# A decoder of two layers on one core: another order for the steps of part one, and another place for two waits

## The reference, cut to what matters

```
x = norm(x + self_attention(x))          # L0: 16 heads of 8, causal
x = norm(x + cross_attention(x, ctx))    # L0X: 8 heads of 16, 64 keys
x = norm(x + experts(x))                 # router, 64 experts, top 6, 64 places each; shared FFN
x = norm(x + self_attention(x))          # L1: 16 heads of 64, causal, biases on q, k, v
x = norm(x + cross_attention(x, ctx))    # L1X: 16 heads of 64
x = norm(x + nested_attention(x))        # L1F: 8 heads of 16, nested widths 128, 64, 32, 16
```

## Time and profile before

| | |
|---|---|
| median of 3 runs | 1771.91 us |
| lowest, highest | 1770.81, 1782.97 us |
| the profiled execution | 1776.66 us |
| its span, first to last instruction | 1774.6 us |
| TensorE busy | 1612.1 us, 91% |
| VectorE busy | 1086.2 us, 61% |
| ScalarE busy | 815.9 us, 46% |
| mean granted TensorE clock | 0.960 |
| part one, experts, part three begin | about 5, 534 and 648 us |

### The profile page before, as it was taken

The page is one execution under the profiler, slowest core; times in us unless marked ns, Lnnn a source line. Parts: engine busy times, 40 slices in busy tenths (PEclk is TensorE's granted clock), DMA queues, the critical chain, the costliest instruction groups (busy, mean ns, idle before and its releaser), DMA issues.

```text
span 1774.6 us, 41025 instructions
## 1 busy us (share of the span) xinstructions
PE 1612.1 (91%) x17280; PEld 1053.8 (59%) x17280; DVE 1086.2 (61%) x2249; ACT 815.9 (46%) x1516; POOL 237.4 (13%) x402
## 2 busy tenths in 40 slices
PE   4899999999978878999999999999999999999985
PEld 1655555555536754675675675675675675675663
DVE  5177777877755454386386387387377277277254
ACT  1456655565542224445345445445445445445423
POOL 1011101110114710011011011011011011011011
PEclk9899999999988879999999999999999999999998
DMA  8331111111118740011011011011011010000000
GB/s 265 151 124 58 53 51 65 53 58 52 54 46 171 117 153 24 20 43 37 16 46 37 7 54 37 2 60 37 1 61 37 2 61 30 8 25 28 5 1 7
DMA packets 64999, 95.68 MB, mean 54 GB/s; under 512 B 9425, under 2 KB 47298, under 8 KB 64083
## 3 DMA queue, kind: packets, MB, share of 16 engines
q1 hardware_dynamic: 61491, 89.20, 15.0%
q0 software_dynamic: 2560, 3.46, 2.2%
q10 hardware_dynamic: 768, 0.40, 0.1%
HBM read 56.03 MB, written 38.80 MB: 53 GB/s over the span
## 4 chain that ended last, share of the span: by engine, by line
PE 72%; DVE 15%; ACT 5%; issue 4%; POOL 2%; DMA 1%; ACTq 0%; DVEq 0%; POOLq 0%; PEldq 0%
PE psum L898 7%; PE psum L804 6%; PE psum L990 6%; PE psum L646 5%; PE psum L885 4%; PE psum L661 3%; PE psum L856 3%; PE psum L671 3%; PE psum L813 3%; ACT prob L1156 3%; DVE kt L1280 3%; DVE va L1280 3%; PE psum L939 2%; PE psum L799 2%; PE psum L703 2%
## 5 line engine op out<-in xcount | busy, mean ns | idle before, releaser
L1156 ACT ACTIVATE prob<-psum 128x1024 f32<-128x1024 f32 (+1 forms) x352 | 322.7, 945 | 329.8 <-PE psum L813 96.0
L1280 DVE TENSOR_REDUCE w_shared<-psum 128x4 bf16<-128x1024 f32 (+1 forms) x160 | 192.8, 1224 | 136.7 <-PE psum L710 94.7
L1458 POOL TENSOR_TENSOR rstd<-moments,eps 128x2 f32<-128x2 f32 x64 | 15.4, 241 | 1005.4 <-DVE moments L1201 1005.4
L1280 DVE TENSOR_REDUCE kt<-psum 128x4 bf16<-128x1024 f32 (+2 forms) x112 | 134.9, 1218 | 15.3 <-PE psum L735 11.5
L804 PE MATMUL psum<-qt,kt 64*128 64x256 f32 x1024 | 131.4, 376 | 0.0
L898 PE MATMUL psum<-prob,v_big 128*64 128x256 f32 x1024 | 124.6, 385 | 0.0
L804 PEld LDWEIGHTS psum<-qt,kt 64*128 64x128 f32 x1024 | 98.6, 189 | 9.9
L939 PE MATMUL psum<-prob,va 128*32 128x256 f32 (+1 forms) x1536 | 95.4, 369 | 1.2 <-ACT prob L1156 1.1
L898 PEld LDWEIGHTS psum<-prob,v_big 128*64 128x64 f32 x1024 | 67.8, 136 | 43.1 <-issue 11.9
L1308 DVE TENSOR_TENSOR qt<-qt,psum 128x1024 f32<-128x1024 f32 x32 | 39.0, 1221 | 85.5 <-PE psum L966 85.0
L1280 DVE TENSOR_REDUCE va<-psum 128x4 bf16<-128x1024 f32 x64 | 76.0, 1215 | 7.3 <-PE psum L747 7.3
(11 more groups left out here) (330 smaller groups left out, 3269.1 us busy)
## 6 DMA issues: line engine op xcount, KB each, us to landing
zd<-kx SPq DMA_DIRECT2D x24, 512.0 KB, 6.0
union<-zd SPq DMA_DIRECT2D x16, 768.0 KB, 4.3
w_late<-ad SPq DMA_DIRECT2D x16, 512.0 KB, 3.7
w_late<-vd SPq DMA_DIRECT2D x16, 512.0 KB, 4.6
ad<-union SPq DMA_DIRECT2D x16, 256.0 KB, 2.1
vd<-union SPq DMA_DIRECT2D x16, 256.0 KB, 2.0
xg<-union SPq DMA_DIRECT2D x16, 192.0 KB, 1.9
w_late<-in_w1T SPq DMA_DIRECT2D x1, 2816.0 KB, 9.8
```

Of the source, the lines that this page charges most:

```text
L1156: nc.scalar.activation(prob_of[a][s][:, slot + 2 * i:slot + 2 * i + 2, 0:n], v.pair(step, i)[:, :, 0:n], ACT.Exp, scale=a.scale).then_inc( ...
L1280: nc.vector.tensor_reduce(dst, src, axis=AX.X, op=ALU.max).then_inc(v.free(step), 1)
```

## The change

Five things change.

1. `TURNS1` is another string; the 94 steps and the streams are the same.
2. The clear of `xt_nested` leaves DVE and the way to `p3_ready`. POOL does it in the first body of part three, in the step W of L1X, just before it waits for the moments there. DVE's wait for `f_stored[2]` goes with it; POOL's waits for all four `f_stored`, which stood at the head of its part three, go to the same place.
3. `b1_v`, the bias of L1's values, has a semaphore of its own, `bias_in`. `weights_in` no longer counts it; DVE waits for `bias_in` at the steps V of L1 in the first body.
4. PE waits for the last shared-FFN copy (`f_z_out`) before part three.
5. Two semaphores, `slots_full` and `masks_made`, are merged into `merged` and `columns_set`; their waits stay.

```
-TURNS1 = ("A B D A C G B A2 B A C B D2 C B G A2 B D C D2 B A C D G C B D C B C D G A D B E D A B2 D G D A E D B "
-          "F B F C E A2 G E F A E A F C B A F G F2 A B G A B A C B A B F A B3 C2 A C F")
+TURNS1 = ("A B D A B C G B A D C B A C D A B A C A D B D2 B C G D A G C A D C3 D G B3 D B E D B A B D G D A E D "
+          "B G E F A2 B F A F C G E A3 F E B F G F A B A C B A B F A B3 C2 A F C F")
...
@@ vector_step, V
                 if a is L1:
+                    if v.first():
+                        dve.wait_ge(bias_in, 16)
...
@@ pool_step, W
                 which = a
+                if a is L1X and v.first():
+                    for p in range(4):
+                        pool.wait_ge(f_stored[p], 16 * len(F_STORES[p]))
+                    nc.gpsimd.memset(xt_nested[s][:, :], 0.0)
                 pool.wait_ge(y.moments_ready[s], v.summed(which, s))
...
-                        sp.dma_start(b1_v, dram("b1_v")).then_inc(weights_in, 16)
+                        sp.dma_start(b1_v, dram("b1_v")).then_inc(bias_in, 16)
...
-        N3 = len(small3) + len(late3) + len(wide3) + 3 * len(NESTED) - 1
+        N3 = len(small3) + len(late3) + len(wide3) - 1 + 3 * len(NESTED) - 1
...
@@ tensor
             experts_tensor(pe)
+            pe.wait_ge(f_z_out, SEQS)
             pe.wait_ge(p3_ready, 1)
...
@@ vector
-            dve.wait_ge(f_stored[2], 16 * len(F_STORES[2]))
-            for s in AB:
-                ms(xt_nested[s][:, :], 0.0)
             dve.wait_ge(weights_in, 16 * N3)
...
@@ gpsimd
             pool.wait_ge(p3_ready, 1)
-            for p in range(4):
-                pool.wait_ge(f_stored[p], 16 * len(F_STORES[p]))
             run_phase(pool, "p3", pool_step)
```

More of the change, by code:

```diff
@@ L1593, in decoder_program @@
         sort_link = sem("sort_link")
-        slots_full = sem("slots_full")
         w13_in = sem("w13_in")
@@ L1615, in decoder_program @@
         p3_ready = sem("p3_ready")
+        bias_in = sem("bias_in")
         def expert_steps():
@@ L1648, in experts_tensor @@
                         last = mm(psum[64 * u:64 * u + 64, Y_BANK, 0:32], final, ident[0:E, u:E:2], start=True, stop=True)
-                    last.then_inc(slots_full, 1)
+                    last.then_inc(merged, 1)
                 elif kind == "F1":
@@ L1772, in experts_vector @@
                 elif kind == "slots":
-                    dve.wait_ge(slots_full, 1)
+                    dve.wait_ge(merged, 2)
                     linked(nc.vector.tensor_copy(slot_key, psum[:, Y_BANK, 0:32]))
@@ L1899, in decoder_program @@
         columns_set = sem("columns_set")
-        masks_made = sem("masks_made")
         cleared = sem("cleared")
@@ L2074, in _ @@
             ts(tri_t[:, 0, :], tri[:, 128:256], -250.0, None, ALU.mult)
-            ts(tri_t[:, 1:4, :], tri_x[:, 1:4, 128:256], -250.0, None, ALU.mult).then_inc(masks_made, 1)
-            dve.wait_ge(masks_made, 1)
+            ts(tri_t[:, 1:4, :], tri_x[:, 1:4, 128:256], -250.0, None, ALU.mult).then_inc(columns_set, 1)
+            dve.wait_ge(columns_set, 3)
             run_phase(dve, "p1", vector_step)
```

## The result

The changed kernel takes 1758.91 us (median of 15 runs, 1751.23 to 1770.45), the kernel before 1773.59 us beside it (15 runs, 1765.11 to 1782.99). The ratio is 0.991, 95% interval 0.989 to 0.993: 0.9% faster. The forecast was 1757, from a sum of -17.1; the medians differ by 14.7. The profiled execution took 1751.36 us, its span 1749.5, mean granted clock 0.982 (before: 0.960).

The account below looks back on a forecast made before the run. TensorE, busy 91% of the span, was taken as the bound, with clock falls in the bodies. Start -1.0, seven bodies -11.5, last body -1.0, seam -3.6: -17.1 from 1776.66, less half of 4.75, gives 1757 us; range 1747 to 1770.

Parts of the forecast that it names:

- The clock: Part one's bodies: with the bunch of small PE steps pulled apart, the clock's fall goes, saving 8.5 us over seven.
- The first rival: The fall stays or comes elsewhere, such as the start of a body: 8.5 us again, 1765.5 us; chance 0.25.
- the rule on transposes: Trainium skill's rule that transposes, such as A1 and A2, don't count as busy work for the clock as other products do.
- First part of a body: From Q of L0 s0 to the second round T: +0.8 us a body, bounds 0 and +1.6.
- VectorE's 1.6 us: Start of a body: two RL steps, not one, precede the masked keys, which start 1.6 us later against PE.
- Second part: From the second round T to A1 of s0: 14.72 to 13.5 us, -1.2 a body, bounds -2.2 and 0.
- The third part: A1 of s0 to P: keeps its order but for the RL steps on DVE; no change counted.
- The start: The 45 steps ahead of body 0: S of s1's 2.28 us wait is eased; -1.0 us, bounds -2 and +1.
- The last body: Paced by the router of s1; RN of s0 now stands ahead of R1's read: -1.0 us, bounds -2 and +1.
- The seam: Way into part three: without DVE's wait for stores and the clear, the first sum starts 3.6 us earlier; bounds -3.6 and -1.
- The 4.75 us: The profiled execution's excess over the median of the runs shown, 1771.91 us; half was taken off the forecast.
- Slower: Rival: VectorE's lateness is passed on and the clock falls twice; bodies of 62.2 us, 1801 us in all; chance 0.06.

Follow-up runs that it names:

- each half: Two kernels: the changed kernel with the old order string, 1772.21 against 1773.53 us (0.999); the kernel before with the new string alone, 1763.15 us (0.995).
- the second pair of profiles: The changed kernel and the kernel before, each run once more unchanged for a second profiled execution: 1754.44 and 1767.54 us.
- the lighter sort: The changed kernel with the second step of each router sort done on 16 columns only: one run, 1749.17 us.
- the sort steps back: The changed kernel with the second RL step right behind the first and the third ahead of W of L0 s0: 1777.9 us, ratio 1.003.
- A1 back: The changed kernel with one step, A1.L0.s1, moved back behind S.L0X and KA, where it stood before: 1789.18 us, ratio 1.010.
- only VW moved: The kernel before with one step, the second VW of s0, moved into the bunch behind R1 of s0: 1765.08 us, ratio 0.994.

## Why the prediction was right

- **The clock**: right. The fall is gone in seven of seven and six of seven bodies. The fourteen bodies average 56.5 us, 1.0 less than those of before, and by the runs of each half this was the larger part of the gain (in the second pair of profiles the seam gave as much). The reason was given too narrowly: VW between S and XT is one of two ways, as the kernels with it alone and without it show. The first rival came true in one body of fourteen, at the start of the body as it said. The new order brings A1 and A2 closer together there, at a clock of 1.00 in the other thirteen; these traces neither bear out the rule on transposes that the rival named nor rule it out.
- **First part of a body**: +1.17 for my +0.8, inside its bounds (0 to +1.6). The mechanism is shown by the lighter sort. A2's new wait is 0.92 us for "about 1". Half of VectorE's 1.6 us was taken as absorbed; a quarter was.
- **Second part**: -1.13 for -1.2. R2 has no wait (404.11 above), the new wait of T is 0.64 for my 0.5, and VW's 1.1 us is confirmed by putting it back (+1.3).
- **The third part** was costed at nothing and took +0.2. So a body without a fall is 56.7, not 56.0; in fact 0.2 us longer than the one of before. This step of the sum failed in size: the order by itself makes a clock-free body no shorter. Seven bodies gave -8.4 for -11.5 (-6.2 in the second pair of profiles), just the fall's 8.5: the first body, with no sort step ahead of its masked keys, makes up for the others.
- **The start** -1.1 for -1.0, but -0.3 in the second pair of profiles; no S behind the first one waits over 1.1 us now, where one had waited 2.28. **The last body** -0.6 for -1.0, of which the router's part came as foreseen: from L of s1 to the last mask it is 511.65 - 503.75 = 7.9 us for 9.5, and the ways to L and from the mask to the merging product are 0.5 us longer each.

```profile
503.75 0.60 DVE L1215 TENSOR_SCALAR union<-v_big,moments_f,rstd_f 128x128 f32<-128x128 f32 x2 [0.50 <-POOL rstd_f L1467]
...
511.23 0.42 DVE L1384 TENSOR_TENSOR qt<-qt 128x256 bf16<-128x256 f32 x1
```

- **The seam** -3.6 as forecast, less 0.5 behind it that I missed: in part three's first norm the moments wait 0.5 us for the statistics ahead of them (the row at 626.35), and from the first sum to PE's first product it is 5.65 or 5.66 us in every profile with the seam's edits, 5.15 or 5.16 in every one without. POOL's clear is 0.32 and 0.31 us in the first body of part three, with over 12 us of idleness behind it, and no other transfer proved last. What I didn't see is that the wait for the stores differs by 3 us between executions of the same kernel.
- **The 4.75 us** between profile and median: 3.1 against the median of 15 runs. It was not falls in bodies, which repeat; the tables and the experts were slow in that execution. That half of it was right to take off was chance.
- **Slower** needed a body of 60.6 us. Two kernels here average 59.4 and 59.3 by just that way, late division and a fall behind it (the sort steps back, A1 back), with single bodies of 60.2 to 62.7. So the chance of 0.06 was low: with A1 in its old place, the late masked keys do this.

The sum of -17.1 asked 3.1 us too much of the bodies; the medians came within 2.4 us of it, the stretches of the two pairs of profiles within 4.0 and 3.8. The mechanism was right; that the figure came so near, 1757 for 1758.91, is in part luck.

## What to carry to other kernels

Where the granted clock falls at the same place of nearly every body, one product on 96 rows, moved from a stretch that is full to one that waits anyhow, can be worth as much as a new order: here 8 us for one string edit. Before making a step wait less by putting another ahead of it, look whether both read the same late tile. And profile a kernel twice before pricing a wait: what repeats belongs to the order; what doesn't can't be put down to an edit from one profile.

## What the runs showed of the hardware

- A fall of the clock half as long cost nothing (only VW moved): 56.50 us a body at 0.97 and at 1.00. It took the place of PE's waits for DVE, 1.29 and 0.56 us in the body at 1.00, 0.23 in the other.
- The kernel before came to its first P at 90.67 us in one execution and at 85.15 in another, and took 102.7 and 95.0 us for the experts: 5.5 and 7.7 us by the execution, in a kernel whose 15 runs spread over 18 us. At the tables the clock goes with it: 0.55 from 70 to 91 us in the first profile, 0.89 from 70 to 85 us in the second.
- A fall needed no long gap ahead in the kernel before (0.37 us); other orders fell behind 1.32, 2.61 and 2.81 us of waiting; one stayed at 1.00 behind the 1.32 us in four bodies of six. Two bodies of the same kernel came to the place with the same rows and waits, and one fell. What decides is not settled by these traces.
